# Gated cross-attention and mixture of experts, one core: the score products as three float32r products of split keys and queries

## What is computed

```python
ln, xn = layer_norm(latents), layer_norm(context)
q = (ln @ Wq) * scale                          # 8 heads of 64
k = concat([rope(xn @ Wk), ln @ Wk])           # 375 + 112 keys
v = concat([xn @ Wv, ln @ Wv])
sim = einsum('bhid,bhjd->bhij', q, k)          # the product that the change touches
out = einsum('bhij,bhjd->bhid', softmax(sim), v)
x = x + tanh(g_xattn) * (out @ Wo)
logits = layernorm(x) @ Wg                     # router: the top 2 of 8 experts
x = x + tanh(g_ffn) * sum over the two of P * (gelu(z @ W1[e] + b1[e]) @ W2[e] + b2[e])
```

## Time and profile before

| | us |
|---|---|
| Median of 3 runs | 540.36 |
| Lowest and highest run | 537.32, 542.07 |
| The profiled execution's own time | 536.03 |
| Its span in the profile | 534.3 |
| First score product starts | 53.13 |

### The profile page before, as it was taken

How to read it: one execution, slowest core, us unless ns; L and a number is a source line. 1 busy time by engine, 2 the same in 40 slices (tenths; PEclk the granted TensorE clock), 3 DMA queues, 4 the chain that set the end, 5 groups by cost and what they waited for, 6 DMA issues and landing times. The chain is left out here.

```text
span 534.3 us, 9451 instructions
## 1 busy us (share of the span) xinstructions
PE 443.3 (83%) x3229; PEld 369.2 (69%) x3229; DVE 288.4 (54%) x698; ACT 296.9 (56%) x652; POOL 191.4 (36%) x208
## 2 busy tenths in 40 slices
PE   2673799999989999998988824259999999999990
PEld 1453476767767676776766621059999999999990
DVE  2684324263443525344346346128888888888850
ACT  3434467666666666667566320037676766776630
POOL 4420163553716345281631034701332222233322
PEclk9976799999999999999999865559999999999996
DMA  7400010000000019994000005285777777784323
GB/s 192 107 29 0 1 30 0 30 3 2 30 0 29 0 39 289 241 253 176 1 1 2 0 11 198 88 276 176 207 200 206 202 207 215 244 255 91 45 29 88
DMA packets 41864, 56.04 MB, mean 105 GB/s; under 512 B 1745, under 2 KB 37153, under 8 KB 41808
## 3 DMA queue, kind: packets, MB, share of 16 engines
q1 hardware_dynamic: 36864, 49.80, 31.1%
q0 software_dynamic: 4960, 5.72, 7.0%
HBM read 40.37 MB, written 16.07 MB: 106 GB/s over the span
## 5 line engine op out<-in xcount | busy, mean ns | idle before, releaser
L1229 POOL DMA_INDIRECT acc_scratch<-yv,xt x28 | 49.1, 1754 | 130.8 <-DVE yv L1430 126.5
L1252 ACT ACTIVATE hf<-ph,b1t 128x256 f32<-128x256 f32 x112 | 47.1, 472 | 49.1 <-PE ph L1497 48.3
L728 DVE TENSOR_REDUCE negmax<-sc 112x1 f32<-112x487 f32 x64 | 42.1, 659 | 44.9 <-PE sc L959 44.9
L553 ACT ACTIVATE prob<-sc,negmax 112x487 f32<-112x487 f32 x64 | 43.6, 681 | 12.5 <-DVE negmax L728 9.4
L984 PEld LDWEIGHTS po<-probt,vals 125*64 125x64 f32 (+1 forms) x512 | 24.8, 137 | 22.7 <-issue 15.4
L561 ACT COPY probt<-pt 125x448 f32<-125x448 f32 x64 | 34.7, 542 | 9.8 <-PE pt L967 9.8
L959 PE MATMUL sc<-keys,queries 64*112 64x488 f32 x128 | 35.3, 629 | 5.6 <-ACT keys L502 3.4
L1412 DVE TENSOR_TENSOR hl<-hf,hh 128x512 fp32r<-128x512 f32 x56 | 38.8, 693 | 1.9
L967 PEld LDWEIGHTS pt<-ident,prob 112*125 112x125 f32 x256 | 36.0, 188 | 4.1
L967 PE MATMUL pt<-ident,prob 112*125 112x112 f32 x256 | 37.9, 272 | 0.0
L1410 DVE CAST hh<-hf 128x512 fp32r<-128x512 f32 x56 | 24.2, 432 | 24.5 <-ACT hf L1252 23.9
(11 more groups left out here) (264 smaller groups left out, 1351.3 us busy)
## 6 DMA issues: line engine op xcount, KB each, us to landing
w_next<-in_L_ffn_W SPq DMA_DIRECT2D x10, 1024.0 KB
rows_scratch<-blank SPq DMA_DIRECT2D x2, 4257.0 KB, 33.2
w_third<-in_L_ffn_W SPq DMA_DIRECT2D x8, 1024.0 KB, 7.7
w1s<-in_L_ffn_W SPq DMA_DIRECT2D x5, 1024.0 KB
w2s<-in_L_ffn_W SPq DMA_DIRECT2D x5, 1024.0 KB, 9.4
xt<-rows_scratch SPq DMA_DIRECT2D x14, 258.0 KB, 2.8
ctx_t<-in_ctx SPq DMA_DIRECT2D x8, 375.0 KB
w1s<-in_L_xattn_Wkv SPq DMA_DIRECT2D x1, 1024.0 KB, 12.9
```

The costliest lines, as they stand in the source:

```text
L553: act.activation(prob[:, h % 2, 0:JA], sc[h % 2][0:M, 0:JA], ACT.Exp, bias=negmax[:, h % 2:h % 2 + 1], accum_out=total[:, p, h:h + 1]).the ...
L728: dve.tensor_reduce(negmax[:, h % 2:h % 2 + 1], sc[h % 2][0:M, 0:JA], AX, ALU.max, negate=True).then_inc(max_done.sem, 1)
L1229: pool.indirect_dma_start(out=acc_dram, out_offset=bass.IndirectOffsetOnAxis(ap=xt[i % 3][:, n, D + 1:D + 2].bitcast(I32), axis=0), in_=yv ...
L1252: last = act.activation(hf[:, n % 3, u], ph[n % 3][:, u * T:(u + 1) * T], ACT.Gelu, bias=b1t[:, col])
```

## The change

`queries` becomes `qh` and `ql`, `keys` becomes `kth` and `ktl`, all float32r. ACT's copies now write the high parts. DVE gets new instructions, `low_query` and `low_key`, which subtract the high part from what still stands in PSUM. Every wait of PE for `keys_done` or `queries_done` becomes one for `ktl_done` or `ql_done`, the low parts. A pair of heads has six float32r products in place of two float32 ones, the two row tiles in turns. `lf`, which lay inside `keys`, gets memory of its own.

```diff
-        queries = sb("queries", [P, 2, HP, M])
+        qh, ql = sb("qh", [P, 2, HP, M], F32R), sb("ql", [P, 2, HP, M], F32R)
...
-        keys = sb("keys", [P, 2, HP, JP])
+        kth, ktl = sb("kth", [P, 2, HP, JP], F32R), sb("ktl", [P, 2, HP, JP], F32R)
...
-                act.copy(keys[:, p, :, j * JR:j * JR + rows],
+                act.copy(kth[:, p, :, j * JR:j * JR + rows],
...
+            def low_query(t, p):
+                dve.wait_ge(qh_done.sem, qh_done.at(t, p, 1))
+                dve.tensor_tensor(ql[:, p], pv[:, 0:HP * M].rearrange("q (a r) -> q a r", a=HP),
+                                  qh[:, p].bitcast(F32), ALU.subtract).then_inc(ql_done.sem, 1)
+
+            def low_key(t, p, n):
+                j = ORDER[n]
+                rows = M if j == JT else JR
+                dve.wait_ge(kth_done.sem, kth_done.at(t, p, n + 1))
+                c = slice(j * JR, j * JR + rows)
+                dve.tensor_tensor(ktl[:, p, :, c],
+                                  key_bank(n)[:, 0:HP * P].rearrange("q (a r) -> q a r", a=HP)[:, :, 0:rows],
+                                  kth[:, p, :, c].bitcast(F32), ALU.subtract).then_inc(ktl_done.sem, 1)
...
                 if s == 3:
+                    low_query(t, p)
                     dve.wait_ge(crstd_done.sem, crstd_done.at(t, p, 1))
                     for j in range(JT):
...
                 if s == 8:
+                    low_key(t, p, 0)
                     if first:
                         rotate(dve, t, p, 0)
...
+                if s == 14:
+                    low_key(t, p, 1)
+                if s == 16:
+                    low_key(t, p, 2)
+                    low_key(t, p, 3)
...
-                    pe.wait_ge(queries_done.sem, queries_done.at(t, p, 1))
+                    pe.wait_ge(ql_done.sem, ql_done.at(t, p, 1))
...
-                pe.wait_ge(keys_done.sem, keys_done.at(t, p, 0))
+                pe.wait_ge(ktl_done.sem, ktl_done.at(t, p, 0))
...
-                    pe.wait_ge(keys_done.sem, keys_done.at(t, p, 1))
+                    pe.wait_ge(ktl_done.sem, ktl_done.at(t, p, 1))
                     transpose_context(t, p, 2)
...
-                    pe.wait_ge(keys_done.sem, keys_done.at(t, p, 2))
+                    pe.wait_ge(ktl_done.sem, ktl_done.at(t, p, 2))
                     transpose_keys(t, p, 2)
...
             def scores(t, p, a):
                 if a == 0:
-                    pe.wait_ge(keys_done.sem, keys_done.at(t, p, NT))
+                    pe.wait_ge(ktl_done.sem, ktl_done.at(t, p, NT))
 
                 pe.wait_ge(exp_done.sem, exp_done.at(t, p, 2 * a))
-                for u in range(2):
-                    r = slice(u * DH, (u + 1) * DH)
-                    pe.matmul(sc[u][0:M, 0:JP], queries[r, p, a], keys[r, p, a], start=True, stop=True,
-                              tile_position=(u * DH, 0)).then_inc(score_done.sem, 1)
+                for n, (q, k) in enumerate(((qh, kth), (qh, ktl), (ql, kth))):
+                    for u in range(2):
+                        r = slice(u * DH, (u + 1) * DH)
+                        last = pe.matmul(sc[u][0:M, 0:JP], q[r, p, a], k[r, p, a], start=n == 0, stop=n == 2,
+                                         tile_position=(u * DH, 0))
+                        if n == 2:
+                            last.then_inc(score_done.sem, 1)
```

More of the change, by code:

```diff
@@ L161, in attention @@
         out_t, heads = sb("out_t", [P, HP, M]), sb("heads", [P, HP, M])
-        lf = [keys[:, 1, n, 0:KD * M].rearrange("p (k m) -> p k m", k=KD) for n in range(2)]
+        lf = [sb(f"lf{n}", [P, KD, M])[:] for n in range(2)]
         tp, pk, pv, po = ps("tp"), ps("pk"), ps("pv"), ps("po")
@@ L190, in attention @@
         qrow_done, qtr_done = tally("qrow_done", 1), tally("qtr_done", 1)
-        queries_done = tally("queries_done", 1)
+        qh_done, ql_done = tally("qh_done", 1), tally("ql_done", 1)
         kproj_done, vproj_done = tally("kproj_done", NT), tally("vproj_done", NT)
@@ L194, in attention @@
         krow_done, klat_done = tally("krow_done", JT), tally("klat_done", 1)
-        ktr_done, keys_done = tally("ktr_done", NT), tally("keys_done", NT)
+        ktr_done, kth_done, ktl_done = tally("ktr_done", NT), tally("kth_done", NT), tally("ktl_done", NT)
         vals_done = tally("vals_done", NT)
@@ L422, in _ @@
         def _(act):
-            for c in (lat_ready, qrow_done, cf_done, ch_done, queries_done, kraw_done, klat_done, keys_done,
+            for c in (lat_ready, qrow_done, cf_done, ch_done, qh_done, kraw_done, klat_done, kth_done,
                       vals_done, exp_done, probt_done, out_done):
@@ L501, in keep_key @@
                 act.wait_ge(score_done.sem, score_done.at(t, p, -H))
-                act.copy(keys[:, p, :, j * JR:j * JR + rows],
+                act.copy(kth[:, p, :, j * JR:j * JR + rows],
                          key_bank(n)[:, 0:HP * P].rearrange("q (a r) -> q a r", a=HP)[:, :, 0:rows]) \
-                    .then_inc(keys_done.sem, 1)
+                    .then_inc(kth_done.sem, 1)
             def prepare(t, p, s, first=False):
@@ L521, in prepare @@
                     act.wait_ge(score_done.sem, score_done.at(t, p, -H))
-                    act.copy(queries[:, p], pv[:, 0:HP * M].rearrange("q (a r) -> q a r", a=HP)) \
-                        .then_inc(queries_done.sem, 1)
+                    act.copy(qh[:, p], pv[:, 0:HP * M].rearrange("q (a r) -> q a r", a=HP)) \
+                        .then_inc(qh_done.sem, 1)
                 if s == 5:
@@ L613, in _ @@
         def _(dve):
-            for c in (cstat_done, cparts_done, cvar_done, cnorm_done,
+            for c in (cstat_done, cparts_done, cvar_done, cnorm_done, ql_done, ktl_done,
                       max_done, inv_done, heads_done, x1_done, ostat_done, oparts_done, ovar_done,
@@ L617, in _ @@
                 c.start(dve)
-            dve.memset(keys[:, :, :, JA:JP], 0.0).then_inc(pad_set, 1)
+            for w in (kth, ktl):
+                dve.memset(w[:, :, :, JA:JP].bitcast(F32), 0.0).then_inc(pad_set, 1)
             dve.memset(prob[:, :, JA:PP], 0.0).then_inc(pad_set, 1)
@@ L842, in other_latents @@
                 if s == H:
-                    pe.wait_ge(pad_set, 2)
+                    pe.wait_ge(pad_set, 3)
                     for done in lf_done:
```

## The result

The changed kernel takes 568.13 us (median of 4 runs, 567.08 to 568.68) against 541.22 for the kernel before in the same session: ratio 1.0504, 95% interval 1.0439 to 1.0568. Slower, as forecast, but the time lies above the forecast's range (its own part was 547 to 563): 27 us were lost and not 17.

A forecast was written before the change was run, and what follows sets the result against it. The prediction took PE as the bound, nearly never idle in steady attention. Its terms -5.1 + 11.2 + 2.1 + 2.0 + 1.3 + 5.5 gave +17.0 us on 536.03, 553.0, or 557.4 on the median; it took 555, range 547 to 563.

The forecast's parts named there:

- its own part: Range of the main forecast without the rivals, 547 to 563 us, holding chance 0.67.
- rival 3: PE's clock falls to half in the new steady stalls, some 3 us each, +18, so 573 us; chance 0.08.
- PE's list is what counts: Steady attention: PE nearly never idle, so work saved there is gain and each new wait on PE full loss.
- The products: Score products: a pair of heads takes 0.85 us instead of 1.01, -5.1 us over 32 pairs.
- rival 2: Score products: weight loads of every pass are exposed, so no saving, 561 us; chance 0.12.
- rival 1: Score products: float32r row tiles don't work at once, six passes in a row, 576 us; chance 0.07.
- The low query: Ahead of the context scaling on DVE: PE's context transpose waits 1.9 us, net 1.6 in seven batches, +11.2 us.
- The low keys: DVE subtractions delaying PE: first low key +2.1 us, second nothing, last ones before the query projection +2.0 us.
- step 8: Place of the first low key in a batch: PE's next context transpose 0.3 us late, seven times, +2.1 us.
- The exponential in the last batch but one: Head 7's row maximum queues behind the last low keys, so PE waits longer for the exponential, +1.3 us once.
- The start-up: First batch: low query delays weights and statistics 4.0 us, low keys delay key transposes 0.7, first scores 0.8; +5.5 us.
- Rival 4: Added DVE work is hidden and PE alone counts, so 532 us profiled, 536 to 537 on the median; chance 0.06.

The follow-up runs named there:

- e4: Changed kernel plus seven spare float32r products on PE between query transposes and context transpose; 556.99 us, ratio 1.0331 to before.
- e10: Changed kernel plus three spare float32r products on PE between query transposes and context transpose; 556.36 us, ratio 1.0312 to before.
- e2: Kernel before with six float32r products per pair in place of two float32 ones, no low parts, scores wrong; 537.25 us, ratio 0.9972 to before.
- e1: Changed kernel with the low query moved behind the scaling of the context on DVE; 548.19 us, ratio 1.0156 to before.
- e6: Changed kernel with the low query behind the scaling and all three products of one row tile before the other's; 548.34 us, ratio 1.0110 to before.
- e3: Changed kernel with all low parts and waits, but scores as two float32 products of the high parts; 565.72 us, ratio 1.0477 to before.

## Why the prediction was wrong, point by point

**The step that failed is the clock behind the new stalls.** The forecast put it at nothing (rival 3, chance 0.08). The runs showed 3.4 us at half clock behind each stall of 1.6 to 1.7 us, 1.38 us a batch and 8.3 in six; with the idle time filled (e4) or shortened to 0.98 us (e10) that cost is gone. The order of two instructions on DVE that makes the stall was forecast, and nearly at its price.

The second trace of before (span 540.7) is the fair partner of the changed kernel's (565.3): 24.6 us apart. First scores 51.55 against 57.87, 6.3 us; from there to the fourth pair 0.5; six batches 189.71 against 205.25, 15.5 us; the rest 2.3. Without the clock's 8.3 the two would be 16.3 apart, where the forecast's sum is 17.0.

The 15.5 us split as follows, from the lengths of six batches in the table:

| Term | runs | six batches, us | forecast for six |
|---|---|---|---|
| Products | e2 less before | -3.5 | -3.8 |
| Low keys, and the low query behind the scaling | e1 less e2 | +2.9 | +3.8 |
| Low query's round trip | e4 less e1 | +7.9 | +9.6 |
| Clock behind the stall | changed less e4 | +8.3 | 0 (rival 3) |

- *PE's list is what counts, waits on it cost in full*: right. DVE's 26 us of added work cost little by their amount; their place cost nearly all.
- *The products, 0.85 us a pair*: right, 0.86 in e6 and 0.15 a pair in e2. The bound with exposed weight loads (rival 2) and the passes in a row (rival 1) are out: the second and third records of a tile start 0.22 us apart and come in pairs. The Trainium skill ("TensorE: Matmul & The Clock Gate", Part 3, the mechanism of tiling) lists that a weight load overlaps with products in flight only when its row group differs. That doesn't hold here: by it a pair would have taken an estimated 1.03 us (the forecast's bound), and it took 0.86. The same part also names a load into a background weight buffer as a second case, which these records fit.
- *The low query*: right in its mechanism. The subtraction takes the 0.62 us read off, and PE idles 1.69 us where I had 1.9. Net it is 1.31 and not 1.6 a batch, because with the low keys in place PE waits 0.37 us for the scaling even when the low query stands behind it (e1), which I hadn't seen.
- *The low keys*: 0.49 us a batch where I had 0.64. Against e2, the query projection idles 1.35 and not 1.16 (forecast 1.50), the context transpose beside step 8 comes 0.41 us behind the product before it and not 0.24 (0.17, forecast 0.3), and the 0.37 for the scaling comes in the place of the 0.27 that e2 waits for ACT at the next context transpose.
- *The exponential in the last batch but one, +1.3 once*: right in kind. PE's longest wait for an exponential went from 1.28 to 2.36 us, +1.1.
- *The start-up, +5.5*: the low query's 4.0 measured about 4.05. The low keys' 1.5 lies inside the 0.7 to 2.3 that two traces of before leave. Starts of one kernel that lie 1.6 us apart don't allow more; that both agree so closely is in part luck.
- *"The clock falls in the new stalls", chance 0.08*: here the forecast failed. I dismissed it because the new stalls, 1.9 us, were shorter than the 2.6 us standstill of the earlier trace rows after which the clock had fallen. That is one observation of where a fall happens. Before's own idle of 1.16 us in every batch, which left the clock at 1.00, is the other; for 1.9 us the rows said neither. The fall came behind every steady stall. Rival 3's price was mis-sized too: 3 us from the six-microsecond stretch of the earlier trace rows, where each fall here lasts 3.4 us and costs 1.38. Forecast plus this term (8.3) is 25 us above the base.
- *The base*: the sum was made against an execution that had its tail at nearly full clock (0.88) and so was 3 to 6 us below a usual one. Between its sum and the median I took 555; on the median it would have been 557.4, and with the clock's term 566.
- *The range*: its high end was added up wrong. The upper bounds as stated (+0.6, 13.3, 3.5, 2.0, 1.3, 6.5) make +27 and not +24. That the time measured against the median of before is also 27 longer is chance, since the clock isn't in that sum.
- *Rival 4, hidden work*: out as it stood, but e1 shows how near it was. With two instructions exchanged, all but 0.37 us of the stall is gone.

Not settled: what decides whether a given 1.69 us stall is followed by a fall (always in the changed kernel, three times of six in e3), and what decides whether the tail of the attention gets full clock.

## What to carry to other kernels

On an in-order engine, place an instruction that waits for another engine behind everything that a third engine is waiting for: one subtraction of 0.62 us ahead of a ready one cost 16 us in six batches, by a round trip over three engines and the clock behind it. When a stall lands on a TensorE that is otherwise nearly always busy, price it twice, once for its length and once for the half clock that may follow. Spare products in the gap show which part is which (here 11 us came back). And take a second trace of the kernel before, before building a sum on the first.

## What the runs showed of the hardware that was not expected

- An idle stretch of 1.69 us on TensorE was followed by 3.4 us at 0.50 of the clock, in every steady batch of the changed kernel and in three of six in e3; with the stretch cut to 0.98 us (e10) the clock stayed at 1.00 for 190 us.
- Two row tiles work at once also when the program issues all three products of one tile before those of the other (e6): the records come out in pairs. Nothing is gained by writing them in turns.
- A float32r product of 488 columns on 64 rows takes its 0.22 us for two tiles at once, so three of them for each of two heads (0.86 us) are just 0.15 us cheaper than the two float32 products (1.01).
